# Token stages: centring and variance as 64x64 blocks, one paired hidden bank, more PSUM banks in the second stage, and other piece orders on TensorE and ScalarE

## The chip, the cores and the metric

The kernel is one program on one core of a Trainium2 chip. The metric is device time in microseconds (us) for one execution, lower is better. The engines are TensorE (PE; its weight loads are PEld), VectorE (DVE), ScalarE (ACT), GpSimd (POOL) and SyncE (SP, which here only issues DMAs). Each engine runs its own instructions in order; semaphores join them.

## The reference

An image tensor x of 4 images, 48 channels, 128 x 128 pixels goes through two layers. Each has a convolution part and then a feed-forward part on tokens (a token is the 48 channels of one pixel):

```python
x = x + _L0_conv_ref(_ln_c(x), ...)
t = _to_tokens(x)
t = t + _L0_ffn_ref(_ln_t(t), L0_ffn_W1, L0_ffn_b1, L0_ffn_W2, L0_ffn_b2)
x = _from_tokens(t, x)
x = x + _L1_conv_ref(_ln_c(x), ...)
t = _to_tokens(x)
t = t + _L1_ffn_ref(_ln_t(t), L1_ffn_W1, L1_ffn_b1, L1_ffn_W2, L1_ffn_b2)

def _ln_t(v, eps=1e-05):
    m = jnp.mean(v, axis=-1, keepdims=True)
    s = jnp.var(v, axis=-1, keepdims=True)
    return (v - m) / jnp.sqrt(s + eps)
def _qlinear(x, W, b):
    y = q_acc(jnp.einsum('bsk,nk->bsn', q_mul(x), q_mul(W)))   # inputs rounded to 5/2-bit floats
    return q_acc(y + q_mul(b))                                 # sums rounded to 5/10-bit floats
# feed-forward: y = _qlinear(relu(_qlinear(x, W1, b1)), W2, b2), 48 -> 192 -> 48
```

## The kernel before

The program runs stages one after another: an expansion, a gated convolution, **token stage 0** (`mix0`), a wavelet part, attention maps, a fusion part, and **token stage 1** (`mix1`). Both token stages are the function `token_mix`. Each ends a convolution (projection and residual), normalises, runs the feed-forward, and stage 0 also makes the channel norm (`_ln_c`) that the next convolution reads. Stage 0 is called with a 96-channel source and is `wide`; stage 1 isn't. Stage 0 lies at about 806 to 1262 us of the span, stage 1 at 2171 to 2534.

A token stage has 64 steps (`2 * N`). A step holds 512 tokens of two images: 48 channels of one image on partitions 0 to 47, of the other on 64 to 111, with a gap of zeros between (`CP` is 112, `PADH` is 64, `NT` is 512, `HID` is 96). A step's work is cut into pieces, and the pieces of a step belong to different pipeline stages. The function `staged` writes each engine's queue: in iteration k it emits, in the order of the list `pieces`, the piece (s, f) for step k - s. So the list is at once a software pipeline and a fixed queue order. The pieces of a step m are:

- `project` (PE, L876/L879 in stage 0, L882 in stage 1) into `x1_bank`, and `add_residual` (DVE, L1034/L1036 or L1039), pipeline stage 0
- `centre_in` (PE, L888: multiply by a matrix that subtracts the mean) and `square("in")` (ACT, L951), stage 0
- `variance("in")` (PE, L906: multiply the squares by a matrix that averages), `root("in")` (ACT: Ln, L958, then Exp, L961), and `quantize_norm` (DVE, L1047: makes the fp8 tile `xq`), stage 1
- `hide(0)`, `hide(1)` (PE, L919: each half of the 192 hidden units, for both images), `round_hidden(0)`, `round_hidden(1)` (ACT, L968: PSUM to the fp16 tile `h16`), `bias_hidden` (DVE, L1053, twice: `hb`), `quantize_hidden` (DVE, L1063: the fp8 tile `hq`), stage 2
- `show` (PE, L931) and `round_shown` (ACT, L974: tile `y`), `add_shown` (DVE, L1069, L1074) and the store, stage 3 in token stage 0 and 4 in token stage 1
- only in token stage 0: `centre_out` (PE, L894) and `square("out")` at 4, `variance("out")`, `root("out")` and `normalise` (DVE, L1083) at 5

An f32 matmul is two MATMUL instructions in the trace, an fp8 matmul one. In the first token stage the bank that `project` fills, `x1_bank`, is also the bank of the variance, and the bank of `show` is that of the outer variance; in the second, `x1_bank` is shared in the same way. So `project` waits on `logged["in"]` (the Ln has read the variance). The hidden banks are two in stage 0 and four in stage 1.

At a stage's start DVE zeroes tiles (L984 to L998) and then sets `prepared`, on which SP waits with its weight loads; after those come the first steps.

The queue order of DVE is in both versions

```python
pieces = [(0, add_residual), (SHOWN, add_shown), (2, bias_hidden), (2, quantize_hidden), (1, quantize_norm)]
if norm_dst is not None:
    pieces.append((5, normalise))
```

## Time and profile before

| what | value |
|---|---|
| runs | 2534.08, 2541.41, 2864.81 us; median 2541.41 |
| profiled execution, own time | 2536.14 us |
| its span | 2534.40 us (1.7 us lie around it) |
| mean granted PE clock | 0.935 of 2.4 GHz |
| busy over the span | PE 2148.1 us, DVE 1439.6, ACT 1151.7, POOL 532.4 |
| token stage 0, 806 to 1262 us | PE 418.5 us busy, ACT 389.0, DVE 347.4 |
| token stage 1, 2171 to 2534.4 us | PE 312.3 us busy, ACT 270.5, DVE 282.1 |

Busy time counts overlapped instructions once. "Idle before" is what an engine waited for in front of an instruction, and what ended the wait. The granted clock is in parts of 2.4 GHz, and has two levels, 1.0 and 0.5.

### The profile page before, as it was taken

What the parts mean: (1) busy time and instruction counts of PE and PEld (TensorE: products, weight loads), DVE (VectorE), ACT (ScalarE), POOL (GpSimd) and SP (SyncE); (2) the same over time, 40 slices, a digit from 0 to 9 for tenths busy, and PEclk for the clock granted to TensorE, in tenths of its full rate; (3) what the DMA queues carried; (4) which work ended last, traced back from release to release, by engine and by line L of the source; (5) the groups of instructions that cost most, each with busy time, mean ns of one, the idle gap of its engine ahead of it and who ended that gap; (6) DMA issues with size and microseconds to landing.
All of it is one profiled execution on the core that took longest, in us unless ns stands there. A gap on an engine that the chain in (4) does not pass through costs nothing. (4 is left out here: it accounts for less than half of the span.)

```text
span 2534.4 us, 69339 instructions
## 1 busy us (share of the span) xinstructions
PE 2148.1 (85%) x25034; PEld 1260.1 (50%) x25034; DVE 1439.6 (57%) x2567; ACT 1151.7 (45%) x2290; POOL 532.4 (21%) x912
## 2 busy tenths in 40 slices
PE   7679949998996999999879999999936777688887
PEld 3345517766784333333346666666614545233332
DVE  3345501111112777777657888787834445588887
ACT  4346522222222888888722323232201111477776
...
GB/s 154 262 256 269 247 295 282 263 264 228 255 216 97 130 150 144 151 141 154 101 113 133 126 134 129 130 129 130 113 112 271 250 247 175 87 112 108 109 110 84
DMA packets 559393, 434.57 MB, mean 171 GB/s; under 512 B 363592, under 2 KB 498432, under 8 KB 555878
## 3 DMA queue, kind: packets, MB, share of 16 engines
...
q8 instruction: 129, 2.11, 0.4%
...
## 5 line engine op out<-in xcount | busy, mean ns | idle before, releaser
L615 PE MATMUL gate_ps<-gate_data,gate_wt 64*64 64x289 f32 x6144 | 391.2, 411 | 29.4 <-issue 22.2
L615 PEld LDWEIGHTS gate_ps<-gate_data,gate_wt 64*64 64x64 f32 x6144 | 307.6, 134 | 114.1 <-issue 45.8
L676 DVE TENSOR_TENSOR gate_out<-gate_gelu,gate_ps 128x578 f32<-128x578 f32 x96 | 72.2, 756 | 375.4 <-PE gate_ps L615 327.1
L968 ACT CAST mix_h<-mix_bank 96x512 f16<-96x512 f32 x512 | 267.6, 592 | 10.3 <-PE mix_bank L919 6.4
L2076 PE MATMUL fus_bank<-fus_xt,fus_taps 64*32 64x256 f32 x3840 | 139.9, 422 | 78.1 <-issue 55.0
L653 ACT ACTIVATE gate_gelu<-gate_ps 128x578 f32<-128x578 f32 x96 | 62.7, 653 | 300.7 <-PE gate_ps L615 275.1
L1053 DVE TENSOR_SCALAR mix_hb<-mix_h,mix_b1q 96x1024 f16<-96x1024 f16 x256 | 122.7, 479 | 98.0 <-ACT mix_h L968 98.0
L919 PE MATMUL mix_bank<-mix_xq,mix_w1q 112*96 112x512 fp8e5 x512 | 143.1, 381 | 34.3 <-ACT mix_h L968 23.0
L1063 DVE CAST mix_hq<-mix_hb 96x2048 fp8e5<-96x2048 f16 x128 | 156.5, 1223 | 21.1 <-DVE mix_hb L1053 19.2
L292 DVE COPY exp_out<-exp_y 128x384 f32<-128x384 f32 x192 | 102.3, 566 | 104.3 <-PE exp_y L255 54.1
L255 PE MATMUL exp_y<-exp_win,exp_xb 48*128 48x192 f32 x1024 | 117.8, 368 | 47.8 <-DVE exp_out L292 29.7
L2076 PEld LDWEIGHTS fus_bank<-fus_xt,fus_taps 64*32 64x32 f32 x3840 | 88.5, 117 | 123.5 <-issue 107.4
L931 PE MATMUL mix_x_bank<-mix_hq,mix_w2q 96*112 96x512 fp8e5 x512 | 135.6, 387 | 6.5 <-DVE mix_hq L1063 4.4
L255 PEld LDWEIGHTS exp_y<-exp_win,exp_xb 48*128 48x128 f32 x1024 | 92.5, 205 | 87.8 <-ACT exp_out L292 52.3
L888 PE MATMUL mix_centre_in<-mix_x,mix_center 112*112 112x512 f32 x256 | 134.3, 607 | 2.1 <-DVE mix_x L1036 1.2
L882 PE MATMUL mix_x_bank<-mix_sc,mix_proj 112*112 112x512 f32 x128 | 86.4, 757 | 58.3 <-ACT mix_logv_in L958 36.8
L906 PE MATMUL mix_x_bank<-mix_sq_in,mix_average 112*112 112x512 f32 x256 | 132.8, 601 | 2.1 <-DVE mix_x L1036 1.2
...
L974 ACT CAST mix_y<-mix_x_bank 112x512 f16<-112x512 f32 x128 | 74.9, 585 | 119.1 <-PE mix_x_bank L931 119.1
L1622 ACT ACTIVATE wav_sg<-wav_small_bank,tab_levels 128x4 f32<-128x4 f32 x48 | 12.7, 264 | 250.7 <-PE wav_small_bank L1527 250.7
L2104 ACT ACTIVATE fus_gate<-fus_bank,fus_bias 128x512 f32<-128x512 f32 x24 | 16.5, 687 | 226.9 <-PE fus_bank L2085 226.9
L1483 PE MATMUL wav_front<-wav_strips,wav_front_w 48*32 48x256 f32 x3840 | 117.0, 382 | 0.0
...
## 6 DMA issues: line engine op xcount, KB each, us to landing
...
```

Of the source, the lines that this page charges most:

```text
L255: mm = pe.matmul(ps_y[h][q % 2][:, O2 * x:O2 * (x + 1)], xb[u][rows, 2 * q + x].rearrange("c s y x -> c (s y x)"), win[rows, :], start=Tru ...
L292: copy(out[u][h][:, :, 2 * q:2 * q + 2], ps_y[h][p][:, 0:2 * O2].rearrange("p (x c) -> p c x", x=2)).then_inc(emptied[h][p], 1)
L615: mm = pe.matmul(banks(a, v)[64 * g:64 * (g + 1), r], wt[q][64 * r:64 * (r + 1), 2 * a + g, n, :], src, start=n == 0, stop=n == 3)
L888: pe.matmul(centre_bank["in"][at.pair][0:CP, :], center[:, :], x1[at.slot][:, :], start=True, stop=True).then_inc(centered["in"], 1)
L906: pe.matmul(var_bank[v][0:CP, :], average[:, :], sq[v][at.pair][:, :], start=True, stop=True).then_inc(var[v], 1)
L919: pe.matmul(bank[(2 * m + h) % len(bank)][0:HID, :], w1q[:, h, m, :], xq[at.pair][:, :], start=True, stop=True).then_inc(hidden, 1)
L931: mm = pe.matmul(x2_bank[0:CP, :], w2q[:, h, m, :], hq[at.pair][:, m, h, :], start=(h + m == 0), stop=(h + m == 2))
L968: act.copy(h16[at.pair][:, m, h, :], bank[(2 * m + h) % len(bank)][0:HID, :]).then_inc(h16_ready, 1)
L1053: relu = dve.tensor_scalar(hb[at.pair][:, m, :, :].rearrange("p h n -> p (h n)"), h16[at.pair][:, m, :, :].rearrange("p h n -> p (h n)"), ...
L1063: dve.tensor_copy(hq[at.pair][:, :, :, :].rearrange("p m h n -> p (m h n)"), hb[at.pair][:, :, :, :].rearrange("p m h n -> p (m h n)"), sa ...
L1483: x = pe.matmul(half(u, r, 0, Q0)[to:to + STRIP], front_w[u][64 * r:64 * r + K0, 5 + dx, :], strips[u][64 * r:64 * r + K0, g, :, dx:dx + S ...
L2076: mm = pe.matmul(part(u, 0)[STRIP * g:STRIP * (g + 1), r], taps[u][rows, ch, m, :], xt[u][rows, ch, g, :, m:m + S0], start=n == 0, stop=n ...
```

## The change

In `token_mix` only:

1. Centring and variance are block-diagonal: the 112x112 matmul becomes two 64x64 matmuls, one for each image, on tiles of the PE array. Centring exchanges the halves (rows 0-63 write partitions 64-127 and the reverse), variance does not, so the two use all four tiles between them. Operand tiles grow to 128 partitions, and the added rows are zeroed once at the start; the fp8 matmuls take 128 rows.
2. `hide(m)` writes both images into one pair of banks, `pair_bank`, for m = 0 and for m = 1. ACT copies them as one 96x1024 instruction. `hide(1)` waits until the copy of `hide(0)` is done, in both stages.
3. Stage 1 has two projection banks and a bank of its own for the variance. `project` there waits on `x1_ready` and not on the Ln; `variance("in")` waits for the Ln of the step before.
4. The order of pieces changes on PE and ACT, in both stages. DVE and SP keep theirs.
5. `show` in stage 0 waits for one Ln of the outer norm more (`n + 2`), and the outer variance for one `y` less.

```diff
-        x1_bank, x2_bank = k.ps("x1_bank"), k.ps("x2_bank")
-        var_bank = {"in": x1_bank, "out": x2_bank}
-        bank = [k.ps(f"bank{j}") for j in range(8 - 2 - 2 * len(norms))]
+        x1_banks, x2_bank = [k.ps(f"x1_bank{u}") for u in range(1 if wide else 2)], k.ps("x2_bank")
+        var_bank = {"in": x1_banks[0], "out": x2_bank} if wide else {"in": k.ps("var_bank")}
+        pair_bank = k.ps("pair_bank", (128, 2 * NT))
...
-                    pe.wait_ge(logged["in"], at.n + 1)
+                    if wide:
+                        pe.wait_ge(logged["in"], at.n + 1)
+                    elif not isinstance(at.n, int) or at.n >= 2:
+                        pe.wait_ge(x1_ready, at.n - 1)
...
+                def exchange(v, at, x):
+                    pe.sem_inc(pe_turn, 1)
+                    pe.matmul(centre_bank[v][at.pair][PADH:128, :], center[0:PADH, 0:PADH], x[0:PADH, :], start=True, stop=True)
+                    pe.matmul(centre_bank[v][at.pair][0:PADH, :], center[PADH:128, PADH:128], x[PADH:128, :],
+                              start=True, stop=True).then_inc(centered[v], 1)
...
-                            pe.wait_ge(y16_ready, capped(at.n + 3, 2 * N) + 1)
+                            pe.wait_ge(y16_ready, capped(at.n + 2, 2 * N) + 1)
...
-                        pe.matmul(var_bank[v][0:CP, :], average[:, :], sq[v][at.pair][:, :],
+                        pe.sem_inc(pe_turn, 1)
+                        pe.matmul(var_bank[v][0:PADH, :], average[0:PADH, 0:PADH], sq[v][at.pair][0:PADH, :], start=True, stop=True)
+                        pe.matmul(var_bank[v][PADH:128, :], average[PADH:128, PADH:128], sq[v][at.pair][PADH:128, :],
                                   start=True, stop=True).then_inc(var[v], 1)
...
-                        if m == 1 and len(bank) == 2:
-                            pe.wait_ge(h16_ready, 4 * at.n + 2)
+                        if m == 1:
+                            pe.wait_ge(h16_ready, 2 * at.n + 1)
...
-                            pe.matmul(bank[(2 * m + h) % len(bank)][0:HID, :], w1q[:, h, m, :], xq[at.pair][:, :],
-                                      start=True, stop=True).then_inc(hidden, 1)
+                            mm = pe.matmul(pair_bank[0:HID, NT * h:NT * (h + 1)], w1q[:, 1 - h, m, :],
+                                           xq[at.pair][:, :], start=True, stop=True)
+                        mm.then_inc(hidden, 1)
...
-                        pe.wait_ge(logged["out"], at.n + 1)
+                        pe.wait_ge(logged["out"], at.n + 2)
...
-                pieces = [(0, project), (SHOWN, show), (2, hide(0)), (2, hide(1)), (1, variance("in")), (0, centre_in)]
+                pieces = [(0, project), (2, hide(0)), (SHOWN, show), (1, variance("in")), (2, hide(1)), (0, centre_in)]
                 if norm_dst is not None:
-                    pieces = [(0, project), (3, show), (2, hide(0)), (4, centre_out), (2, hide(1)), (1, variance("in")), (5, variance("out")), (0, centre_in)]
+                    pieces = [(0, project), (5, variance("out")), (2, hide(0)), (3, show), (4, centre_out), (1, variance("in")), (2, hide(1)), (0, centre_in)]
...
-                        for h in range(2):
-                            act.wait_ge(hidden, 4 * at.n + 2 * m + h + 1)
-                            act.copy(h16[at.pair][:, m, h, :], bank[(2 * m + h) % len(bank)][0:HID, :]
-                                     ).then_inc(h16_ready, 1)
+                        act.wait_ge(hidden, 2 * at.n + m + 1)
+                        act.copy(h16[at.pair][:, m, :, :].rearrange("p h n -> p (h n)"), pair_bank[0:HID, :]
+                                 ).then_inc(h16_ready, 1)
...
-                pieces = [(SHOWN, round_shown), (2, round_hidden(0)), (2, round_hidden(1)), (1, root("in")),
-                          (0, square("in"))]
+                pieces = [(2, round_hidden(0)), (SHOWN, round_shown), (1, root("in")), (2, round_hidden(1)), (0, square("in"))]
                 if norm_dst is not None:
-                    pieces = [(3, round_shown), (2, round_hidden(0)), (4, square("out")), (2, round_hidden(1)), (1, root("in")), (5, root("out")), (0, square("in"))]
+                    pieces = [(5, root("out")), (2, round_hidden(0)), (3, round_shown), (4, square("out")), (1, root("in")), (2, round_hidden(1)), (0, square("in"))]
...
+                dve.memset(center[:, :], 0.0)
+                dve.memset(average[:, :], 0.0)
+                for x in x1 + x2 + xq:
+                    dve.memset(x[96:128, :], 0.0)
+                for x in hq:
+                    dve.memset(x[96:128].rearrange("p m h n -> p (m h n)"), 0.0)
```

## Rows read from the trace of the kernel before

**Rows 1.** The chain that ended last, 2200 to 2534 us, its shares by line

```profile
by line: ACT mix_h L968 30.5%; PE mix_x_bank L882 23.1%; PE mix_x_bank L931 15.9%; issue 14.5%; ACT mix_logv_in L958 10.2%; ACT mix_y L974 1.3%; ACTq L967 1.2%; DVE mix_hq L1063 0.7%; DVE mix_hb L1053 0.4%; DVE mix_xq L1047 0.4%; PE mix_ban
```

**Rows 2.** Windows: length, busy PE, PEld, DVE, ACT, POOL, granted clock, DMA share, GB/s

```profile
806.00:1262.00 456.00, 418.45 (x1522) 171.96 (x1522) 347.43 (x573) 389.04 (x698) 0.00 (x0) 0.99 0.73 139
2171.00:2534.40 363.40, 312.25 (x896) 123.81 (x896) 282.11 (x448) 270.54 (x512) 0.00 (x0) 0.97 0.40 103
2510.00:2520.00 10.00, 8.22 (x28) 3.57 (x28) 7.80 (x13) 7.94 (x16) 0.00 (x0) 1.00 0.16 45
2520.00:2530.00 10.00, 4.14 (x13) 1.62 (x12) 6.63 (x12) 4.54 (x9) 0.00 (x0) 0.70 0.14 40
```

**Rows 3.** Timeline, token stage 0, PE: start, length, line, tiles, [idle before <- releaser]

```profile
1004.11 0.60 PE L919 MATMUL mix_bank<-mix_xq,mix_w1q 112*96 112x512 fp8e5 x2 [0.44 <-ACT mix_h L968]
...
1005.41 1.02 PE L906 MATMUL mix_x_bank<-mix_sq_out,mix_average 112*112 112x512 f32 x2
1006.27 1.02 PE L888 MATMUL mix_centre_in<-mix_x,mix_center 112*112 112x512 f32 x2
1007.22 0.98 PE L876 MATMUL mix_x_bank<-mix_sc,mix_proj 96*48 96x448 f32 x4
```

**Rows 4.** Timeline, token stage 0, ACT, one step

```profile
1002.41 0.58 ACT L974 CAST mix_y<-mix_x_bank 112x512 f16<-112x512 f32 x1 [0.67 <-PE mix_x_bank L931]
...
1009.35 0.58 ACT L974 CAST mix_y<-mix_x_bank 112x512 f16<-112x512 f32 x1 [0.67 <-PE mix_x_bank L931]
```

**Rows 5.** Timeline, token stage 1, PE

```profile
2354.67 1.03 PE L931 MATMUL mix_x_bank<-mix_hq,mix_w2q 96*112 96x512 fp8e5 x4
2355.54 1.03 PE L919 MATMUL mix_bank<-mix_xq,mix_w1q 112*96 112x512 fp8e5 x4
...
2358.90 1.33 PE L882 MATMUL mix_x_bank<-mix_sc,mix_proj 112*112 112x512 f32 x2 [0.61 <-ACT mix_logv_in L958]
2360.06 1.03 PE L931 MATMUL mix_x_bank<-mix_hq,mix_w2q 96*112 96x512 fp8e5 x4
```

**Rows 6.** Timeline, token stage 1, ACT

```profile
2355.74 0.58 ACT L974 CAST mix_y<-mix_x_bank 112x512 f16<-112x512 f32 x1 [1.14 <-PE mix_x_bank L931]
2356.22 2.04 ACT L968 CAST mix_h<-mix_bank 96x512 f16<-96x512 f32 x4
2358.13 0.72 ACT L958 ACTIVATE mix_logv_in<-mix_x_bank,mix_eps 112x512 f32<-112x512 f32 x1
2358.88 0.63 ACT L961 ACTIVATE mix_rstd_in<-mix_logv_in 112x512 f32<-112x512 f32 x1
```

**Rows 7.** Timeline, last steps of token stage 1, PE, ACT and DVE

```profile
2517.29 1.03 PE L919 MATMUL mix_bank<-mix_xq,mix_w1q 112*96 112x512 fp8e5 x4 [1.77 <-DVE mix_xq L1047]
...
2517.71 2.04 ACT L968 CAST mix_h<-mix_bank 96x512 f16<-96x512 f32 x4 [0.89 <-PE mix_bank L919]
...
2519.78 0.48 DVE L1053 TENSOR_SCALAR mix_hb<-mix_h,mix_b1q 96x1024 f16<-96x1024 f16 x1 [0.49 <-ACT mix_h L968]
...
2520.45 1.22 DVE L1063 CAST mix_hq<-mix_hb 96x2048 fp8e5<-96x2048 f16 x1 [0.18 <-DVE mix_hb L1053]
...
2521.59 0.68 DVE L1047 TENSOR_TENSOR mix_xq<-mix_centre_in,mix_rstd_in 112x512 fp8e5<-112x512 f32 x1
...
2522.42 1.03 PE L919 MATMUL mix_bank<-mix_xq,mix_w1q 112*96 112x512 fp8e5 x4 [2.37 <-DVE mix_xq L1047]
```

**Rows 8.** Groups by form: line, tiles, count, busy us, mean ns, idle before

```profile
L615 PE MATMUL gate_ps<-gate_data,gate_wt 64*64 64x289 f32 x6144 | 391.2, 411 | 29.4 <-issue 22.2 <-ACT gate_wt L648 4.1 <-DVE gate_out L676 3.1
L968 ACT CAST mix_h<-mix_bank 96x512 f16<-96x512 f32 x512 | 267.6, 592 | 10.3 <-PE mix_bank L919 6.4
L637 ACT ACTIVATE gate_stage<-gate_ps,gate_maps 96x1024 f32<-96x1024 f32 x10 | 10.2, 1107 | 5.9 <-PE gate_ps L578 5.9
L629 ACT ACTIVATE gate_hid<-gate_ps,gate_maps 128x512 f32<-128x512 f32 x2 | 1.4, 687 | 8.9 <-PE gate_ps L568 8.9
L993 DVE MEMSET mix_rs<- 32x512 f32 x4 | 1.9, 485 | 0.5
```

More of the change, by code:

```diff
@@ L721, in token_mix @@
         rs = [k.sb(f"rs{u}", [CP, NT]) for u in U]
-        x1 = [k.sb(f"x1{u}", [CP, NT]) for u in range(KEPT)]
+        x1 = [k.sb(f"x1{u}", [128, NT]) for u in range(KEPT)]
         norms = ("in", "out") if norm_dst is not None else ("in",)
-        sq, logv, rstd = ({v: [k.sb(f"{name}_{v}{u}", [CP, NT]) for u in U] for v in norms}
+        sq, logv, rstd = ({v: [k.sb(f"{name}_{v}{u}", [128, NT]) for u in U] for v in norms}
                           for name in ("sq", "logv", "rstd"))
-        xq = [k.sb(f"xq{u}", [CP, NT], F8) for u in U]
+        xq = [k.sb(f"xq{u}", [128, NT], F8) for u in U]
         h16 = [k.sb(f"h16{u}", [HID, 2, 2, NT], F16) for u in U]
         hb = [k.sb(f"hb{u}", [HID, 2, 2, NT], F16) for u in U]
-        hq = [k.sb(f"hq{u}", [HID, 2, 2, NT], F8) for u in U]
+        hq = [k.sb(f"hq{u}", [128, 2, 2, NT], F8) for u in U]
         y16 = [k.sb(f"y16{u}", [CP, NT], F16) for u in U]
         yb = [k.sb(f"yb{u}", [CP, NT], F16) for u in U]
-        x2 = [k.sb(f"x2{u}", [CP, NT]) for u in U]
+        x2 = [k.sb(f"x2{u}", [128, NT]) for u in U]
         xn = [k.sb(f"xn{u}", [CP, 4 * 2 * XW]) for u in U] if norm_dst is not None else None
@@ L838, in store_norm @@
                     for h in range(2):
-                        rows = slice(PADH * h, PADH * h + C)
+                        rows = slice(PADH * (1 - h), PADH * (1 - h) + C)
                         def keep(y, first, n):
@@ L893, in centre_out @@
                     pe.wait_ge(xn_ready, at.n + 1)
-                    pe.matmul(centre_bank["out"][at.pair][0:CP, :], center[:, :], x2[at.pair][:, :],
-                              start=True, stop=True).then_inc(centered["out"], 1)
+                    exchange("out", at, x2[at.pair])
                 def variance(v):
                     def piece(at):
-                        if v == "in":
+                        if v == "in" and not wide:
+                            pe.wait_ge(logged["in"], at.n + FREE["in"])
+                        elif v == "in":
                             pe.wait_ge(x1_ready, capped(at.n + 2, 2 * N))
                         else:
-                            pe.wait_ge(y16_ready, capped(at.n + 3, 2 * N) + 1)
+                            pe.wait_ge(y16_ready, capped(at.n + 2, 2 * N) + 1)
                             if isinstance(at.n, int):
@@ L950, in piece @@
                         act.wait_ge(centered[v], at.n + 1)
-                        act.activation(sq[v][at.pair][:, :], centre_bank[v][at.pair][0:CP, :], ACT.Square).then_inc(squared[v], 1)
+                        act.activation(sq[v][at.pair][:, :], centre_bank[v][at.pair][:, :], ACT.Square).then_inc(squared[v], 1)
                     return piece
@@ L957, in piece @@
                         act.wait_ge(var[v], at.n + 1)
-                        act.activation(logv[v][at.pair][:, :], var_bank[v][0:CP, :], ACT.Ln,
+                        act.activation(logv[v][at.pair][0:CP, :], var_bank[v][0:CP, :], ACT.Ln,
                                        bias=eps[0:CP, m:m + 1]).then_inc(logged[v], 1)
                         act.wait_ge(logged[v], at.n + 1 + FREE[v])
-                        act.activation(rstd[v][at.pair][:, :], logv[v][at.pair][:, :], ACT.Exp, scale=-0.5).then_inc(rooted[v], 1)
+                        act.activation(rstd[v][at.pair][0:CP, :], logv[v][at.pair][0:CP, :], ACT.Exp, scale=-0.5).then_inc(rooted[v], 1)
                     return piece
@@ L997, in _ @@
                         dve.memset(sc[u][0][32:64, :], 0.0)
-                dve.memset(x1_bank[32:64, :], 0.0).then_inc(prepared, 1)
+                for x in x1_banks:
+                    last = dve.memset(x[32:64, :], 0.0)
+                last.then_inc(prepared, 1)
                 dve.wait_ge(weights_in, 16 * (9 if wide else 12))
@@ L1032, in outer @@
                             return x[:, :].rearrange("c (y v x) -> c y v x", y=4, x=P8)[:, :, :, 0]
-                        dve.tensor_tensor(inner(x1[at.slot]), x1_bank[0:CP, 0:cut].rearrange(
+                        dve.tensor_tensor(inner(x1[at.slot][0:CP]), x1_banks[0][0:CP, 0:cut].rearrange(
                             "c (y x v) -> c y x v", y=4, v=BX), inner(rs[at.pair]), ALU.add)
-                        add = dve.tensor_tensor(outer(x1[at.slot]), x1_bank[0:CP, cut:NT].rearrange(
+                        add = dve.tensor_tensor(outer(x1[at.slot][0:CP]), x1_banks[0][0:CP, cut:NT].rearrange(
                             "c (y v) -> c y v", v=BX), outer(rs[at.pair]), ALU.add)
                     else:
-                        add = dve.scalar_tensor_tensor(out=x1[at.slot][:, :], in0=x1_bank[0:CP, :],
+                        add = dve.scalar_tensor_tensor(out=x1[at.slot][0:CP, :], in0=x1_banks[at.pair][0:CP, :],
                                                        scalar=pbias[0:CP, 0:1], in1=rs[at.pair][:, :],
@@ L1062, in quantize_hidden @@
                     dve.sem_inc(dve_turn, 1)
[L1063 removed]
+                    dve.tensor_copy(hq[at.pair][0:HID].rearrange("p m h n -> p (m h n)"),
                                     hb[at.pair][:, :, :, :].rearrange("p m h n -> p (m h n)"), saturate=False
```

30 lines of the change are left out of this document (14 added, 16 removed).

## Prediction

> **What bounds the kernel now.** I began with the busy time in windows [rows 2]. In token stage 0 PE is busy 418 of 456 us and ACT 389; in token stage 1 PE 312 of 363, DVE 282, ACT 271. No engine is full, so each stage runs at the length of a closed loop of waits, and the reader should look for the idle time that comes back in every step. A step of stage 0 lasts 1009.35 - 1002.41 = 6.94 us [rows 4]; 64 of them are 444 us. In each, PE idles 0.44 us for ACT's copy of the hidden half [rows 3] and ACT 0.67 us for `show` [rows 4]. A step of stage 1 lasts 2360.06 - 2354.67 = 5.39 us [rows 5], in all 345 us. There `project` waits 0.61 us for the Ln [rows 5], because the two share a bank, and ACT waits 1.14 us for `show` [rows 6]. The chain of waits names that loop: copies of the hidden half 30.5%, `project` 23.1%, `show` 15.9%, Ln 10.2% [rows 1].
>
> **A second loop, close behind.** The last steps of stage 1 have no `project` left, so they show what comes next [rows 7]: hide starts at 2517.29 and again at 2522.42, 5.13 us apart, and what it waited for is `xq`. The loop is: hide to first copy 0.42; four copies 2.04; 0.03; first `hb` start to `hq` start 0.67; `hq` to `xq` 1.14; `xq` to the next hide 0.83. It sums to 5.13. It is closed because DVE's queue has `xq` of step m+1 behind `hb` and `hq` of step m, and the change leaves DVE's queue alone. So in stage 1 this loop had 0.26 us of slack; removing the first loop alone buys at most that.
>
> **Part 1, removed waits.** In stage 1 `project` no longer waits for the Ln. The gain is 0.26 us a step, 17 us in all, if the second loop stays at 5.13. In stage 0 that wait stays.
>
> **Part 2, the paired copy.** Four copies of 512 become two of 1024. From 512 to 1024 columns an ACTIVATE grows from 687 to 1107 ns [rows 8], 420 ns. A 592 ns copy [rows 8] becomes 1.01 us. The next ACT instruction starts some 0.10 us before an end (2355.74 + 0.58 against 2356.22 [rows 6]). Two pairs cost 2.04 now and 1.93 then: ACT gains 0.1 us a step. In exchange a copy waits for both matmuls, 0.22 us more (half of the 0.43 that a hide of two takes, 0.87 for four [rows 5]).
>
> **Part 3, tiles.** Two 64x64 matmuls replace one 112x112, each as long as before (0.86 us from 1005.41 to 1006.27 [rows 3]). Side by side the pair costs 0.86, in turn 1.72. The gate convolution also uses 64x64 tiles: 6144 instructions in 391 us [rows 8], 64 ns each, where 289 columns at the pace of the centring (512 in 0.43) last 242 ns. So nearly four tiles run at once there, and I take side by side; that also lets the outer centring and the inner variance overlap in stage 0. A change of array shape costs 0.10 us: `centre_in` to `project` takes 0.95 where like shapes take 0.86 [rows 3]. Stage 0 goes from two changes to six. These terms matter only where they lie on the loop.
>
> The Trainium skill, TensorEngine Tiling, Restrictions and Gotchas, Gotcha 1, speaks against this: different row tiles cannot access the same PSUM bank simultaneously, and here both halves of a pair write one bank. No row here shows two row tiles in one bank. By that rule the sum is that of the second rival below.
>
> **Part 4, the orders.** This decides. The second copy, on which `hb` waits, moved behind the root on ACT, while `hide(1)` moved behind `show` and the variance on PE. I walk the second loop again, with 0 at the start of `hide(0)`.
>
> Stage 1: two matmuls, so the copy starts at 0.42 [rows 7] + 0.22 = 0.64 and lasts 1.01, ACT is free at 1.55. `show` starts at 0.43, its result is read at 0.43 + 1.07 = 1.50 (2354.67 to 2355.74 [rows 5, 6]), so `y` runs from 1.55 and ACT is free at 2.03. The variance starts at 0.43 + 0.87 + 0.10 = 1.40 and can be read 1.07 later, so the Ln starts at 2.47. Ln to Exp takes 0.75 (2358.13 to 2358.88), Exp to the next 0.63 - 0.10 = 0.53 [rows 6]: the second copy starts at 3.75 and ends at 4.76. `hide(1)` was done by 2.9. Then as now 0.03 + 0.67 + 1.14 + 0.83 = 2.67 to the next hide [rows 7]. The loop is 7.4 us where the step now takes 5.39. PE has only about 4.9 us of work in it (`project` 1.16 [rows 5], hides 0.87, `show` 0.87, two pairs 1.72, changes 0.3) and can't shorten it.
>
> Stage 0: copy from 0.64 to 1.65. `show`, then a change: centring starts at 1.40, read at 2.47. `y` is over before; the outer square runs from 2.47 (0.53 to the next), Ln from 3.0 (variance beside the centring, ready by then), Exp, second copy at 3.0 + 0.75 + 0.53 = 4.28, end 5.29, and 2.67 behind it: 7.9 to 8.0. I take 7.9 against 6.94. The new `show` wait on the outer Ln doesn't bind: that Ln is first on ACT, its variance right behind `project`, before a hide that waits for `xq`. Behind the waiting hide on PE stand `show`, both norms and `centre_in`; ACT's copy waits for it and so does everything behind that.
>
> **Sum.** Stage 1: 64 x (7.4 - 5.39) = 129 us. Stage 0: 64 x (7.9 - 6.94) = 61 us. The zeroing lies in front of the weight loads, which wait for it, so nothing hides it. A 32x512 MEMSET takes 485 ns [rows 8], some 0.55 with what follows. Stage 0 adds eight of that size (`x1`, `x2`, two `hq` of 2048 bytes), stage 1 thirteen (eight `x1`, `x2`, `hq`, one bank); the fp8 `xq` and the two matrices are a quarter of it, four in each stage: 21 x 0.55 + 8 x 0.15 = 13 us. The clock: stage 1 will have one PE gap of some 2.3 us a step. In the tail of before, gaps of 1.77 and 2.37 [rows 7] lie in a window granted 1.00 and the next is 0.70 [rows 2], one level of 2.4 and one of 1.2 GHz. A fall in a step doubles hide, `show` and variance, up to 2.2 us. Between none and all 64 steps that is 0 to 140 us; since a single gap of 2.37 did not bring it down at once, I take 10. The sum against the profiled 2536.1 is 2536 + 129 + 61 + 13 + 10 = 2749 us; the median of the runs lies 5 above the profiled one, so 2754.
>
> **Rivals.**
> - *The clock falls in most steps of stage 1.* For it: the 0.70 window [rows 2]. Against it: gaps of 2 us are filled in both neighbours by 4.9 us of work. 48 steps x 2.0 = 96 us in place of 10: 2840.
> - *The two tiles of a pair take turns.* For it: no row has that case. Against it: the gate's tiles [rows 8], and `project`'s four instructions of 448 columns in 0.98 us [rows 3] where in turn they need 1.5, though those halves differ in columns only. Stage 1: the variance is ready 0.86 later, 8.3 us a step. Stage 0: centring and variance in turn, ready at 3.3 and 5.0, then Ln, Exp, copy and the rest, about 10.0. 64 x (2.9 + 3.1) = 384 us in place of 190: 2948.
> - *Faster: the second loop doesn't close.* If ACT's second copy ended within 2.7 us of `hide(0)`'s start in stage 1, as the four copies do now (2.46 [rows 7]), the stage would be limited by PE at 4.9 and stage 0 by ACT at 6.94 - 0.67 - 0.1 = 6.2. 64 x (0.5 + 0.75) = 79 us less and 13 for the zeroing: 2475. It needs Ln, Exp and `y`, 1.8 us, off the way between the two copies. The printed order puts them there, so this is only a misreading of the queue.
> - *Within 2%*: the loop closes, but steps overlap more than my walk allows by half or more in both stages.
>
> **How the numbers follow.** Forecast 0.68, clock 0.12, turns 0.10, faster 0.06, within 2% 0.04. Two percent is 51 us, which is about what a measurement of this kernel can tell from no change (two runs of before lie 7 us apart, one 320 above). The forecast's own range is 2715 to 2795, from 0.3 us a step either way in 128 steps; to hold 8 in 10 it reaches over the clock rival: 2690 to 2855. Slower 0.90, within 2% 0.04, faster 0.06.
>
> **What would show each step.** In stage 1, hides `hide(0)` to `hide(0)` 7.4 us apart, each released by `xq`, with PE idle some 2.3 us; `hb`'s second half waiting about 1 us or more for the copy; the copy at 1.01 us. In stage 0, 7.9 us a step, also released by `xq`. No wait of `project` on the Ln in stage 1. Centring, two tiles, in about 1.1 us in all, not 1.9. The granted clock of stage 1 tells the first rival. The prediction is wrong if DVE isn't what `hide(0)` waits for, or if the gap between the two copies on ACT is far from 2.1 us.

## The result, and the profile after

| kernel | median us | runs |
|---|---|---|
| before | 2537.74 | 2527.68 to 2864.81, 4 runs |
| after | 2758.23 | 2754.97 to 2765.58, 4 runs |

The ratio is 1.0892, with a 95% interval of 1.0857 to 1.0927. The change makes the kernel 8.9% slower. One run of before, at 2864.81 us, lies 13% above its other three, and the ratio leaves it out. The profiled execution of after took 2754.97 us, its span 2753.2: 218.8 us more than the span of before.

I place that difference by counting steps. A step is the distance between two `y` copies on ACT; "typical" is the median distance, "mean" is first `y` to last `y` over 63, the shorter last steps included. The two differ where some steps are held up and others are not.

| | stage 0 typical / mean | stage 1 typical / mean |
|---|---|---|
| before | 6.93 / 6.91 us | 5.39 / 5.32 us |
| after | 7.89 / 8.05 us | 7.43 / 7.56 us |

First `y` to last `y` is 506.9 us in stage 0 of after (825.69 to 1332.62), 435.1 before: 72 more. In stage 1 it is 476.2 (2271.49 to 2747.70) against 335.1: 141 more. The wait in front of a stage's first `project` grew by 5.4 us in stage 0 and 7.6 us in stage 1 (from 19.34 and 21.51 to the 24.75 and 29.07 below). Sum 226; the other stages came out 7 us shorter.

Windows of after, over both token stages and over one typical step of stage 1 (columns as in [rows 2]):

```profile
800.00:1330.00 530.00, 412.99 (x2028) 128.38 (x2028) 340.47 (x569) 376.95 (x568) 0.00 (x0) 0.97 0.64 120
2250.00:2753.00 503.00, 365.46 (x1148) 100.86 (x1146) 281.21 (x447) 270.64 (x384) 0.00 (x0) 0.93 0.28 73
2454.99:2462.42 7.43, 5.30 (x18) 1.51 (x19) 4.40 (x8) 4.20 (x6) 0.00 (x0) 1.00 0.31 83
```

Against [rows 2]: ACT's and DVE's busy time in stage 1 is what it was (270.5 and 282.1), while the stage is 140 us longer. These two got no more work; they wait. PE's busy time rose from 312 to 365 us, for changes of array shape and matmuls at the lower clock, and still PE is idle for 138 of 503 us. The third line shows how much: in a step of 7.43 us PE works 5.30, DVE 4.40, ACT 4.20.

Timeline of after, PE: the first `project` of each stage, some of stage 0, and one step of stage 1. It answers to [rows 3] and [rows 5]:

```profile
802.72 1.73 PE L879 MATMUL mix_x_bank<-mix_sc,mix_proj 96*48 96x448 f32 x4 [24.75 <-DMA mix_sc<-g]
...
1059.60 0.64 PE L891 MATMUL mix_centre_out<-mix_x,mix_center 64*64 64x512 f32 x1
1059.60 0.64 PE L892 MATMUL mix_centre_out<-mix_x,mix_center 64*64 64x512 f32 x1
1059.77 0.61 PE L916 MATMUL mix_x_bank<-mix_sq_in,mix_average 64*64 64x512 f32 x1
1059.77 0.64 PE L917 MATMUL mix_x_bank<-mix_sq_in,mix_average 64*64 64x512 f32 x1
...
1066.09 0.60 PE L930 MATMUL mix_pair_bank<-mix_xq,mix_w1q 128*96 128x512 fp8e5 x2 [1.65 <-DVE mix_xq L1065]
...
1071.78 0.98 PE L879 MATMUL mix_x_bank<-mix_sc,mix_proj 96*48 96x448 f32 x4 [1.41 <-DMA mix_sc<-g]
...
2245.52 2.02 PE L885 MATMUL mix_x_bank<-mix_sc,mix_proj 112*112 112x512 f32 x2 [29.07 <-DMA mix_sc<-mixed]
...
2454.99 0.60 PE L930 MATMUL mix_pair_bank<-mix_xq,mix_w1q 128*96 128x512 fp8e5 x2 [2.13 <-DVE mix_xq L1065]
2455.43 1.03 PE L943 MATMUL mix_x_bank<-mix_hq,mix_w2q 128*112 128x512 fp8e5 x4
2456.39 0.64 PE L916 MATMUL mix_var_bank<-mix_sq_in,mix_average 64*64 64x512 f32 x1
...
2457.39 0.63 PE L930 MATMUL mix_pair_bank<-mix_xq,mix_w1q 128*96 128x512 fp8e5 x2
2457.96 0.64 PE L891 MATMUL mix_centre_in<-mix_x,mix_center 64*64 64x512 f32 x1
...
2458.96 1.33 PE L885 MATMUL mix_x_bank<-mix_sc,mix_proj 112*112 112x512 f32 x2
2462.42 0.60 PE L930 MATMUL mix_pair_bank<-mix_xq,mix_w1q 128*96 128x512 fp8e5 x2 [2.13 <-DVE mix_xq L1065]
```

In the last line the reader is to see the loop closing: PE has been idle for 2.13 us, and what it waited for is `xq`. `project` (2458.96) no longer waits for the Ln, as the change intends [rows 5]. Where that 7.43 us goes is on ACT (answering to [rows 6]) and on DVE (answering to [rows 7]):

```profile
2455.63 1.01 ACT L979 CAST mix_h<-mix_pair_bank 96x1024 f16<-96x1024 f32 x1 [2.81 <-PE mix_pair_bank L930]
2456.54 0.58 ACT L985 CAST mix_y<-mix_x_bank 112x512 f16<-112x512 f32 x1
2457.51 0.69 ACT L970 ACTIVATE mix_logv_in<-mix_var_bank,mix_eps 112x512 f32<-112x512 f32 x1 [0.39 <-PE mix_var_bank L917]
2458.23 0.63 ACT L973 ACTIVATE mix_rstd_in<-mix_logv_in 112x512 f32<-112x512 f32 x1
2458.77 0.99 ACT L979 CAST mix_h<-mix_pair_bank 96x1024 f16<-96x1024 f32 x1
...
2459.79 0.48 DVE L1071 TENSOR_SCALAR mix_hb<-mix_h,mix_b1q 96x1024 f16<-96x1024 f16 x1 [1.16 <-ACT mix_h L979]
...
2460.45 1.22 DVE L1081 CAST mix_hq<-mix_hb 96x2048 fp8e5<-96x2048 f16 x1 [0.18 <-DVE mix_hb L1071]
2461.60 0.68 DVE L1065 TENSOR_TENSOR mix_xq<-mix_centre_in,mix_rstd_in 112x512 fp8e5<-112x512 f32 x1
```

From the second `hide` (2457.39) on, its bank could be copied at 2458.03, but ACT starts at 2458.77, since Ln and Exp are ahead of it in the queue and the Ln waits for the variance. Measured from 2454.99, the chain stands at 0.64 (first copy), 1.55 (`y`), 2.52 (Ln), 3.78 (second copy), 4.80 (`hb`), 5.46 (`hq`), 6.61 (`xq`), 7.43 (next `hide`).

### The profile page after: what moved, and what is told of

Same layout as the page of the kernel before. It is cut to its first block and busy times, and to the rows that moved or that the text cites. A ratio compares the mean times of both kernels' runs of the same rounds, so it can differ in the third digit from the quotient of the medians.

```text
span 2753.2 us, 70702 instructions
## 1 busy us (share of the span) xinstructions
PE 2193.6 (80%) x25802; PEld 1201.5 (44%) x25802; DVE 1451.6 (53%) x2596; ACT 1141.8 (41%) x2034; POOL 531.6 (19%) x912
## 5 line engine op out<-in xcount | busy, mean ns | idle before, releaser
L615 PEld LDWEIGHTS gate_ps<-gate_data,gate_wt 64*64 64x64 f32 x6144 | 315.6, 134 | 101.1 <-issue 40.7
L979 ACT CAST mix_h<-mix_pair_bank 96x1024 f16<-96x1024 f32 x256 | 255.4, 998 | 221.8 <-PE mix_pair_bank L930 221.8
L930 PE MATMUL mix_pair_bank<-mix_xq,mix_w1q 128*96 128x512 fp8e5 x512 | 166.3, 408 | 207.3 <-DVE mix_xq L1065 206.6
L930 PEld LDWEIGHTS mix_pair_bank<-mix_xq,mix_w1q 128*96 128x96 fp8e5 x512 | 43.5, 124 | 444.6 <-issue 444.5
L943 PE MATMUL mix_x_bank<-mix_hq,mix_w2q 128*112 128x512 fp8e5 x512 | 139.0, 396 | 6.4 <-DVE mix_hq L1081 3.5
L891 PE MATMUL mix_centre_in<-mix_x,mix_center 64*64 64x512 f32 x256 | 140.8, 631 | 2.3 <-DVE mix_x L1054 1.3
L892 PE MATMUL mix_centre_in<-mix_x,mix_center 64*64 64x512 f32 x256 | 140.9, 631 | 0.0
L1087 DVE TENSOR_SCALAR mix_yb<-mix_y,mix_b2q 112x512 f16<-112x512 f16 x128 | 45.1, 353 | 166.6 <-ACT mix_y L985 166.6
```

The lines of the kernel that those rows point to most:

```text
L615: mm = pe.matmul(banks(a, v)[64 * g:64 * (g + 1), r], wt[q][64 * r:64 * (r + 1), 2 * a + g, n, :], src, start=n == 0, stop=n == 3)
L891: pe.matmul(centre_bank[v][at.pair][PADH:128, :], center[0:PADH, 0:PADH], x[0:PADH, :], start=True, stop=True)
L892: pe.matmul(centre_bank[v][at.pair][0:PADH, :], center[PADH:128, PADH:128], x[PADH:128, :], start=True, stop=True).then_inc(centered[v], 1)
L930: mm = pe.matmul(pair_bank[0:HID, NT * h:NT * (h + 1)], w1q[:, 1 - h, m, :], xq[at.pair][:, :], start=True, stop=True)
L943: mm = pe.matmul(x2_bank[0:CP, :], w2q[:, h, m, :], hq[at.pair][:, m, h, :], start=(h + m == 0), stop=(h + m == 2))
L979: act.copy(h16[at.pair][:, m, :, :].rearrange("p h n -> p (h n)"), pair_bank[0:HID, :]).then_inc(h16_ready, 1)
```

## The experiments

Their steps and times; the ratio is to the runs of before on the same chip. e1 to e4 ran on one chip (before 2536.20 us there), e5 to e9 on a second (2531.43), e10 to e13 on a third (2538.49), so times of different groups are compared by their ratios or by their steps. The kernels e5, e6 and e11 ran once and have no interval. The intervals of e2, e3 and e12 lie clear of 1 but reach over 2%.

| kernel | stage 0 typical / mean | stage 1 typical / mean | us | ratio |
|---|---|---|---|---|
| e1_xq_before_hq | 7.25 / 7.95 | 6.03 / 5.95 | 2646.65 | 1.0432 (1.0380 to 1.0483) |
| e2_xq_first | 7.08 / 7.95 | 5.13 / 5.07 | 2588.85 | 1.0211 (1.0153 to 1.0269) |
| e3_old_orders | 6.55 / 6.90 | 6.11 / 6.11 | 2596.75 | 1.0234 (1.0185 to 1.0283) |
| e4_tiles_only | 6.61 / 6.92 | 5.39 / 5.32 | 2542.36 | 1.0029 (1.0005 to 1.0053) |
| e5_extra_ahead | 10.0 / 9.74 | 8.97 / 8.72 | 2939.37 | |
| e6_extra_behind | 8.24 / 8.30 | 7.43 / 7.62 | 2780.73 | |
| e8_xq_first_late_store | 7.26 / 7.23 | 5.13 / 5.07 | 2543.7 | 1.0052 (1.0036 to 1.0068) |
| e9_tiles_late_store | 6.61 / 6.59 | 5.39 / 5.33 | 2525.76 | 0.9977 (0.9959 to 0.9996) |
| e10_before_late_store | 6.93 / 6.88 | 5.39 / 5.32 | 2532.93 | 0.9975 (0.9953 to 0.9998) |
| e11_ahead_project_twice | 10.0 / 9.78 | 9.11 / 8.87 | 2954.85 | |
| e12_best_old_stage0 | 6.55 / 6.54 | 4.80 / 4.82 | 2479.99 | 0.9774 (0.9746 to 0.9802) |
| e13_new_stage0 | 6.03 / 6.03 | 4.80 / 4.79 | 2442.6 | 0.9631 (0.9598 to 0.9664) |

**e1 and e2: take `hq`, then `hb` too, off the loop.** Both are after with another queue order on DVE. In e2 `hide` also waits until ACT has copied the bank's earlier contents, which in after follows from `xq`.

```diff
 # e1
-pieces = [(0, add_residual), (SHOWN, add_shown), (2, bias_hidden), (2, quantize_hidden), (1, quantize_norm)]
+pieces = [(0, add_residual), (SHOWN, add_shown), (2, bias_hidden), (1, quantize_norm), (2, quantize_hidden)]
 # e2
+pieces = [(0, add_residual), (SHOWN, add_shown), (1, quantize_norm), (2, bias_hidden), (2, quantize_hidden)]
 # e2, in hide(0)
+elif not isinstance(at.n, int) or at.n >= 1:
+    pe.wait_ge(h16_ready, 2 * at.n)
```

Expected of e1:

> The changed kernel with one edit: on DVE xq of the next step is made ahead of the hidden cast hq of this one. Loop theory (hide, copy, root, copy, hb, hq, xq, hide): the loop loses hq's 1.14 us and the 0.2 us that hq waits for hb, so stage 1 goes from 7.43 to about 6.0 us a step, and stage 0 from 8.0 to 7.2 to 7.4; in all 2755 - 64 x (1.4 + 0.6 to 0.8) = 2615 to 2630 us. Rival, tiles and changes of array shape on PE: no piece of PE changes, so 2755 stays. Rival, the shared pair of banks: the two hides and the two copies are as before, so 2755 stays.

Expected of e2:

> The changed kernel with xq of the next step ahead of both hb and hq on DVE, and a wait of hide(0) for the second copy of the step before, which was implied until now. Loop theory: what is left of the loop is hide, copy, root, copy, hide: 4.8 us in stage 1, where PE's own work of about 4.9 to 5.0 then sets the step; stage 0 about 7.1. In all 2755 - 64 x (2.45 + 0.9) = 2540 us, so as fast as the kernel before. Rival, tiles on PE: 2755. Rival, the shared pair of banks: 2755 or more, since one more wait on it is written out.

Timeline of e1, PE, stage 1:

```profile
2401.32 0.60 PE L930 MATMUL mix_pair_bank<-mix_xq,mix_w1q 128*96 128x512 fp8e5 x2 [0.73 <-DVE mix_xq L1065]
...
2407.35 0.60 PE L930 MATMUL mix_pair_bank<-mix_xq,mix_w1q 128*96 128x512 fp8e5 x2 [0.73 <-DVE mix_xq L1065]
```

One swap on DVE takes 1.40 us off a step: PE's idle time falls by the same amount, 2.13 to 0.73. `xq` now starts 0.41 us behind `hb` where it started 1.81 behind it (2461.60 - 2459.79): the 1.15 of `hq`, and the 0.25 that `hq` waits for `hb` and `xq` doesn't. In e2 nothing is left of the loop in stage 1. Windows of e2:

```profile
2380.00:2500.00 120.00, 120.00 (x424) 36.77 (x420) 100.71 (x164) 98.19 (x142) 0.00 (x0) 1.00 0.43 115
```

PE is busy for 120.00 of 120 us and the step is 5.13, PE's own work. Neither PE's nor ACT's order was touched, so the loss of stage 1 is the loop through DVE's queue, and nothing else. But both kernels came out above what was expected of them (2646.65 against 2615 to 2630, 2588.85 against 2540), because stage 0 took 7.95 us a step in the mean. Its steps alternate there, in e2 6.95 and mostly 8.7 to 9.5 us, and the median (7.25, 7.08) lies at the short ones. Something else holds stage 0. Timeline of e2, stage 0, all engines:

```profile
1056.02 0.98 PE L879 MATMUL mix_x_bank<-mix_sc,mix_proj 96*48 96x448 f32 x4 [1.46 <-DMA mix_sc<-g]
...
1059.11 1.04 PE L945 MATMUL mix_x_bank<-mix_hq,mix_w2q 128*112 128x512 fp8e5 x4 [0.43 <-ACT mix_logv_out L972]
1060.32 0.58 ACT L987 CAST mix_y<-mix_x_bank 112x512 f16<-112x512 f32 x1
1060.93 0.35 DVE L1089 TENSOR_SCALAR mix_yb<-mix_y,mix_b2q 112x512 f16<-112x512 f16 x1 [1.90 <-ACT mix_y L987]
1061.51 0.69 DVE L1094 TENSOR_TENSOR mix_x<-mix_yb,mix_x 112x512 f32<-112x512 f16 x1 [0.22 <-DVE mix_yb L1089]
1062.37 0.86 SPq L834 DMA_DIRECT2D x<-mix_x  x2
...
1063.51 0.88 SPq L843 DMA_DIRECT2D xp<-mix_xn  x2
1064.59 0.34 SPq L801 DMA_DIRECT2D mix_sc<-g  x1
...
1072.18 1.36 PE L879 MATMUL mix_x_bank<-mix_sc,mix_proj 96*48 96x448 f32 x4 [1.70 <-DMA mix_sc<-g]
```

Read downwards it is a third loop. `project` (1056.02) holds up `show`, since the outer variance stands behind it on PE (1057.05), ACT's Ln reads that (1058.17), and `show` waits 0.43 us for the Ln. That is the wait that the change added; it costs 1.0 us in all in stage 0 of after, but 9.2 us in e2, both between 830 and 1240 us. SP issues, in a fixed order, the stores of `x` and `xp` and then the next source load. The store waits for `add_shown` (`mix_x`, 1062.20), so the load of a later source is issued only at 1064.59, takes 7.6 us to land and be seen, and `project` (1072.18) waits for it. From `project` to that `project` are 16.16 us. One load brings the source of two steps: 8.08 us a step. The waits of e2 between 830 and 1240 us add `project`'s up to (total, times, longest):

```profile
PE mix_x_bank L879 <- DMA mix_sc<-g: 36.0, 25, 1.9
```

After has the same wait (24.7 us in 22 waits between 830 and 1240 us; the line at 1071.78 above is one).

**e8, e9, e10: move the store behind in SP's queue.** In e2, e4 (below) and before, `store_x2` of token stage 0 goes one pipeline stage later.

```diff
-staged(sp, 2 * N, KEPT, [(0, load), (SHOWN + 1, store_x2)] + [(7, store_norm)] * wide, LEAD)
+staged(sp, 2 * N, KEPT, [(0, load), (SHOWN + (2 if wide else 1), store_x2)] + [(7, store_norm)] * wide, LEAD)
```

> e2_xq_first with one edit: in stage 0, SP's store of x2 is one iteration later in its queue (stage 5 for stage 4), so that the load of the next source tile is not queued behind a store that waits for y. New theory for stage 0 (third loop, over two steps: project, show, y, x2, SP's stores, source load 7.5 us, project): stage 0 goes from 7.95 to about 7.1 us a step, 50 us less than e2_xq_first, near 2538 us; stage 1 stays at 5.13. Rival, DMA bandwidth bounds stage 0 (busy share 0.65): nothing changes, 2589. Rival, the later store delays DVE's next x2: slower than e2_xq_first.

> e4_tiles_only with the same later store of x2. In e4_tiles_only most steps of stage 0 take 6.61 us, but the mean is 6.92, with waits for the source load. Third-loop theory: the mean comes down to about 6.6, 64 x 0.3 = 20 us less than e4_tiles_only, near 2522 us, a little faster than the kernel before. Rival, DMA bandwidth: it stays at 2542.

> The kernel before with the later store of x2 in stage 0 alone. If the source load is only just in time before (issued at 1013.82, landing 7.2 us later, project at 1021.1), its other loop (copy of the hidden half, y) sets 6.93 us a step: no change, 2531 us, within 0.3%. Rival: the store is what holds stage 0 before too: up to 0.3 us a step, 20 us faster.

In e8 the wait of `project` on the load is gone, and the mean step falls from 7.95 to 7.23; the steps no longer alternate, and the typical one is 7.26. That is 45 us in 63 steps; the ratios, 1.0211 and 1.0052, say 40. In e9 the mean goes from 6.92 to 6.59. In e10, before with the late store, it goes from 6.91 to 6.88 only, 2 us in all: before's loop of 6.94 us [rows 4] was just as long as this one, so shortening one of them was worth next to nothing there. What sets the 7.26 us of e8, 0.33 over before, was not taken apart.

The third loop was there before, hidden, and the change lengthened it to 8 us. In before the load is issued 6.60 us after `project` (1007.22 in [rows 3]):

```profile
1013.82 0.34 SPq L801 DMA_DIRECT2D mix_sc<-g  x1
```

In e2 it is issued 8.57 us after it (1056.02 to 1064.59), 2 us more for two steps. `show` starts 1.0 us behind `project` in before and 3.1 in e2, with the outer variance, a `hide` and the wait for the Ln between them. With the orders and waits of before and the new tiles (e3, e4) the mean is 6.90 and 6.92; no run parts the order on PE from that on ACT and from the added wait.

**e3: the old orders with the new tiles and banks.** After, with the lists of PE and ACT from before and their waits.

```diff
 # PE, stage 1
-pieces = [(0, project), (2, hide(0)), (SHOWN, show), (1, variance("in")), (2, hide(1)), (0, centre_in)]
+pieces = [(0, project), (SHOWN, show), (2, hide(0)), (2, hide(1)), (1, variance("in")), (0, centre_in)]
 # ACT, stage 1
-pieces = [(2, round_hidden(0)), (SHOWN, round_shown), (1, root("in")), (2, round_hidden(1)), (0, square("in"))]
+pieces = [(SHOWN, round_shown), (2, round_hidden(0)), (2, round_hidden(1)), (1, root("in")), (0, square("in"))]
...
```

> The changed kernel with the piece orders of before on PE and ACT, and the two waits that belong to them; 64x64 blocks, pair of banks, bank split of stage 1 stay. Loop theory: the copies are close together again. Stage 1: PE waits in hide(1) for the first copy, so the loop is copy, hide, copy, hb, hq, xq, hide: 6.2 us a step (7.43 in the changed kernel, 5.39 before). Stage 0 about 7.0. In all 2755 - 64 x (1.2 + 1.0) = 2615 us. Rival, tiles and shape changes: it stays near 2755. Rival, shared pair: it keeps most of the loss, and in stage 0 too.

Timeline of e3, PE, stage 1:

```profile
2400.00 0.60 PE L930 MATMUL mix_pair_bank<-mix_xq,mix_w1q 128*96 128x512 fp8e5 x2 [0.57 <-DVE mix_xq L1065]
2401.80 0.60 PE L930 MATMUL mix_pair_bank<-mix_xq,mix_w1q 128*96 128x512 fp8e5 x2 [1.19 <-ACT mix_h L979]
...
2406.11 0.60 PE L930 MATMUL mix_pair_bank<-mix_xq,mix_w1q 128*96 128x512 fp8e5 x2 [0.57 <-DVE mix_xq L1065]
```

Back to back, the second `hide` has to wait 1.19 us until ACT has read the one pair of hidden banks: 1.80 from `hide` to `hide`, 0.64 to the copy, 1.01 of copy, 2.67 to the next `hide` [rows 7], which is 6.12; measured 6.11. So the old orders are better than the new ones here by 1.3 us, and still worse than before by 0.7 because of the single pair. Stage 0, which had two hidden banks already, gains 0.38 in the typical step but nothing in the mean (6.90), since every second step waits for its source load.

**e4: only the tiles.** Before, with the 64x64 blocks, the 128-row operands and the zeroing; the edit in words:

```diff
-centre and variance: one 112x112 matmul
+centre: two 64x64 matmuls that exchange the halves; variance: two that don't
+dve.memset of the added rows; w1q[:, 1 - h], 128-row fp8 operands
```

> The kernel before with the 64x64 blocks, 128-row operands and their zeroing alone; banks, 512-column copies and orders are those of before. Loop theory: only changes of array shape that lie on a loop count, 0.1 us each: none in stage 1 (5.4 us a step), one in stage 0 (7.0), and 13 us for the zeroing: 2537 + 13 + 6 = 2556 us, within 1% of before. Rival, tiles are what costs: most of the 217 us, over 2650.

The typical step of stage 0 was 6.61, shorter than the 7.0 expected; PE's timeline in e4 says why:

```profile
1000.80 0.64 PE L911 MATMUL mix_x_bank<-mix_sq_in,mix_average 64*64 64x512 f32 x1
1000.81 0.64 PE L912 MATMUL mix_x_bank<-mix_sq_in,mix_average 64*64 64x512 f32 x1
1000.83 0.64 PE L888 MATMUL mix_centre_in<-mix_x,mix_center 64*64 64x512 f32 x1
1000.84 0.64 PE L889 MATMUL mix_centre_in<-mix_x,mix_center 64*64 64x512 f32 x1
...
1001.71 0.59 PE L911 MATMUL mix_x_bank<-mix_sq_out,mix_average 64*64 64x512 f32 x1
```

The queue holds inner variance, outer variance, inner centring. The centring, on the two tiles that the variances do not use, runs with the inner variance, 0.03 us behind it, and the outer variance, which stands ahead of it in the queue, follows 0.88 us later. All regular steps of e4 have this, with 0.76 to 0.88 us between the two. Three pairs take the time of two. The gain of 0.32 a step is then lost to the source load (mean 6.92), and stage 1 is unchanged, its loops being elsewhere. What is left of e4 against before is the zeroing: 13 us by the waits, 1 to 13 by the ratio. e9, without the third loop, should be 63 x (6.88 - 6.59) = 18 us faster than e10 by its steps, less 13 of zeroing; the ratios (0.9977 and 0.9975, each about 0.002 either way) cannot tell the 5 us that are left from nothing.

**e5 and e6: one more DVE instruction, in the loop or behind it.** A second copy of `xq`'s instruction writes to a tile that nobody reads, ahead of `xq` (e5) or right behind it (e6). All other work is that of after.

```diff
+spare = k.sb("spare", [128, NT], F8)
 ...
+dve.tensor_tensor(spare[0:CP, :], centre_bank["in"][at.pair][0:CP, :], rstd["in"][at.pair][0:CP, :], ALU.mult, saturate=False)
```

> The changed kernel with one DVE instruction more in each step: the operation that makes xq is done once more into a spare tile, directly ahead of xq. Loop theory: the instruction lies on the loop in stage 1, so the step grows by its 0.60 us, from 7.43 to 8.03. Stage 0 grows too, by 0.3 to 0.6. In all 2755 + 38 + 20 to 38 = 2810 to 2830 us. Rival, the load of stage 1 on DVE as a whole or PE's tiles set the step: DVE is busy under 60% there, so nothing is added, or as much as in e6_extra_behind.

> The changed kernel with the same extra DVE instruction directly behind xq. Loop theory: in stage 1 PE has xq already and goes on, and DVE waits over 1 us later in the step anyway, so the step stays at 7.43. In stage 0 it delays the residual add and the store, so 0 to 0.4 us a step. In all 2755 to 2780 us. Rival, DVE's load as a whole: the same growth as e5_extra_ahead.

DVE is busy 4.40 of 7.43 us, so a theory of busy time says that neither costs anything. Behind `xq` (e6), stage 1 keeps its 7.43, and stage 0 grows by 0.35 in the typical step. Ahead of it, the step at full clock is 8.02. Timeline of e5, PE:

```profile
2514.78 0.60 PE L931 MATMUL mix_pair_bank<-mix_xq,mix_w1q 128*96 128x512 fp8e5 x2 [2.56 <-DVE mix_xq L1068]
...
2515.22 1.03 PE L944 MATMUL mix_x_bank<-mix_hq,mix_w2q 128*112 128x512 fp8e5 x4
...
2522.80 0.69 PE L931 MATMUL mix_pair_bank<-mix_xq,mix_w1q 128*96 128x512 fp8e5 x2 [2.73 <-DVE mix_xq L1068]
2523.29 1.91 PE L944 MATMUL mix_x_bank<-mix_hq,mix_w2q 128*112 128x512 fp8e5 x4
...
2532.47 0.60 PE L931 MATMUL mix_pair_bank<-mix_xq,mix_w1q 128*96 128x512 fp8e5 x2 [2.73 <-DVE mix_xq L1068]
```

0.59 us more, as `xq` itself needs from start to next start (2461.60 to 2462.20). But two steps in three of e5, from `hide` to `hide`, are like the second one, 9.1 to 9.7 us, with `show` and its neighbours at half pace (1.91 us where the step before has 1.03). So the expectation of 2810 to 2830 us failed: against the profiled run of after the kernel lost 184 us and not the 75 that 128 x 0.59 makes. Windows of e5, stage 1:

```profile
2400.00:2920.00 520.00, 365.75 (x1049) 97.16 (x1048) 290.74 (x466) 249.31 (x353) 0.00 (x0) 0.88 0.24 65
```

The granted clock is 0.88 against after's 0.93, and 0.85 between 850 and 1240 us of stage 0, against 0.99. In stage 1 the rest of the loss is that: the first rival of the prediction, real in this kernel. In stage 0 the typical step grew from 7.89 to 10.0, and how much of that is the clock was not measured apart.

**e11: fill the gap.** e5, with `project` of stage 1 issued twice into the same bank with the same values.

```diff
-mm = pe.matmul(x1_banks[at.pair][0:CP, :], proj[:, :], ...)
+for _ in range(2):
+    mm = pe.matmul(x1_banks[at.pair][0:CP, :], proj[:, :], ...)
```

> e5_extra_ahead with the projection matmul of stage 1 issued twice (the second writes the same values over the first): 1.16 us more work for PE in each step, in its idle gap of 2.7 us. Clock theory: e5_extra_ahead lies over its walk (8.03 us a step in stage 1, most steps measured about 9.0) because PE falls to 1.2 GHz after that gap in nearly every step. With the gap filled to about 1.6 us the granted clock of stage 1 rises from 0.88 to over 0.97 and the mean step falls from 8.72 to about 8.1, 40 us less in all, near 2900 us, although PE does more. Rival, the extra length of e5_extra_ahead has another cause, such as DVE or a bank: no change, 2939, or 64 x 1.16 = 74 us more if PE's work lies on the loop.

Timeline of e11, PE, and its window of stage 1:

```profile
2611.99 0.60 PE L932 MATMUL mix_pair_bank<-mix_xq,mix_w1q 128*96 128x512 fp8e5 x2 [1.65 <-DVE mix_xq L1069]
...
2620.01 1.06 PE L932 MATMUL mix_pair_bank<-mix_xq,mix_w1q 128*96 128x512 fp8e5 x2 [1.65 <-DVE mix_xq L1069]
```

```profile
2400.00:2920.00 520.00, 424.68 (x1143) 120.94 (x1141) 287.52 (x460) 243.48 (x343) 0.00 (x0) 0.88 0.24 65
```

The gap is 1.65, shorter than after's 2.13, PE is busy 425 of 520 us, and the clock is still 0.88. The expectation, over 0.97 and near 2900 us, failed. So the length of this gap alone is not what decides. What makes the clock fall in most steps here, and in about every fourth step of stage 1 in after, stays open.

**e12 and e13: a version that beats both.** e12 is e3's stage 0 (tiles, the old queue orders) with the late store; in stage 1 after's banks and orders with `xq` first on DVE as in e2, and 112x112 blocks without zeroing. e13 is e12 with stage 0 written anew:

```diff
 # PE, stage 0
-[(0, project), (3, show), (2, hide(0)), (4, centre_out), (2, hide(1)), (1, variance("in")), (5, variance("out")), (0, centre_in)]
+[(5, variance("out")), (4, centre_out), (0, project), (2, hide(0)), (3, show), (2, hide(1)), (1, variance("in")), (0, centre_in)]
 # ACT, stage 0
+[(5, root("out")), (2, round_hidden(0)), (4, square("out")), (3, round_shown), (2, round_hidden(1)), (1, root("in")), (0, square("in"))]
 # DVE, stage 0
+[(0, add_residual), (5, normalise), (3, add_shown), (2, bias_hidden), (1, quantize_norm), (2, quantize_hidden)]
```

> A kernel put together from what the runs showed. Stage 0: 64x64 blocks, paired copies, the piece orders of before and the later store (6.55 us a step in most steps of e3_old_orders). Stage 1: pair of banks, bank split and piece orders of the change, xq first on DVE, but 112x112 matmuls and no zeroing for them, so four changes of array shape less, 0.2 to 0.3 us of PE's 5.13 us in e2_xq_first: 4.85 to 4.95 us. In all 2531 + 13 - 7 - 64 x (0.38 + 0.5) = 2481 us, 2% faster than before. Rival, the loops of stage 0 come back through the DMA queue: 2505.

> e12_best_old_stage0 with other orders in stage 0. PE: outer variance, outer centring, project, hide(0), show, hide(1), inner variance, inner centring. ACT: outer root, copy, outer square, y, copy, inner root, inner square. DVE: residual add, normalise, add of y, hb, xq, hq. Both pairs of norms overlap on PE's tiles; by the walk the engines allow 6.0 us a step. The source load allows about 9.7 us and SP's issues for two steps, some 6.2 a step. So 6.2 to 6.6 us: 2465 to 2481 us. Rival, y is late for the store and the load: slower than e12_best_old_stage0.

e12 takes 2480.0 us (0.9774), as expected; e13 takes 2442.6 us (0.9631, 0.9598 to 0.9664), better than the 2465 to 2481 expected, because its stage 0 runs at 6.03 us a step and not at 6.2 to 6.6. In stage 1 the step is 4.80, 0.33 less than e2's 5.13: the same orders without tiles. There PE is the bound, and four changes of array shape less give about 0.1 each; the fp8 operands have fewer rows there too, which no run parts from it. Windows of e13:

```profile
820.00:1215.00 395.00, 366.30 (x2008) 122.44 (x2000) 334.94 (x568) 370.78 (x571) 0.00 (x0) 0.99 0.83 158
2120.00:2440.00 320.00, 303.93 (x888) 118.49 (x886) 275.32 (x446) 268.22 (x383) 0.00 (x0) 0.99 0.43 115
```

In stage 1 PE is nearly full, in stage 0 PE and ACT are both over 90% busy: little is left for the loops to cost.

## Why the prediction was right

It said 2754 in a range of 2690 to 2855; measured 2758.23. That the two are 4 us apart is partly luck: in the sum below, terms that came out too small and 7 us that nobody explained cancel. The mechanism, though, is the one it named. By its own steps:

- *The second loop.* The walk of stage 1 had 0.64, 1.55, 2.47, 3.75, the `hb` at 4.79 and 7.4 at the end; the trace has 0.64, 1.55, 2.52, 3.78, 4.80 and 7.43. e1, e2, e5 and e6 show in stage 1 that it is the loop: what is taken off its path comes off the step, an instruction added on it comes on in full, and beside it costs nothing. Its term of 129 us holds (63 x 2.04). PE's own work, put at 4.9 us a step, is 5.13 in e2; it lay under the loop and did not count.
- *Part 1.* Right, and worth nothing in this order: `project` lost its wait and started none of the work earlier that counts. Whether the separate bank pays where the second loop is cut (e2, e12) no run shows by itself.
- *Part 2.* The paired copy was put at 1.01; the mean of 256 is 0.998. What it costs beside its length was seen only partly: a single pair of banks makes `hide` wait for the copy as soon as the two are near each other (1.19 us in e3). The new order hides this.
- *Part 3.* Both halves of a pair start together, 0.01 us apart in most steps and 0.04 at most, though both write one bank, each its own partitions: `mix_x_bank` at 1059.77, and `mix_var_bank`, where the whole pair takes 1.00 with its change of shape (2456.39 to 2457.39). Centring, two tiles, takes 1.00 (2457.96 to 2458.96), predicted 1.1. In stage 0 outer centring and inner variance, four tiles, take 1.17 together (1059.60 to 1060.77). The Trainium skill, TensorEngine Tiling (Array Packing), Restrictions and Gotchas, Gotcha 1, says that different row tiles cannot access the same PSUM bank simultaneously. The trace does not agree: here they do, and the pair takes 1.00 us and not the 1.7 of two in turn.
- *Stage 0, the term that was mis-sized.* "I take 7.9": the typical step is 7.89, but the mean is 8.05, and 72 us came instead of 61. What was missing in the walk is the third loop, through SP's queue. The prediction weighed the wait of `show` on the outer Ln, rightly for after, and named what stands behind it on PE and ACT. It did not follow `show` through `y`, `x` and the store to the source load. In after the second loop hides most of it (8.05, against 7.95 where the second loop is cut), which is why the miss stayed small. After itself was not run with the late store, so that the source loads are what is over 7.89 is read from the waits. In e1 and e2 it took nearly all that stage 0 would have gained: mean 7.95 where e8 has 7.23.
- *The zeroing.* 13 us predicted, 5.4 + 7.6 = 13.0 measured in the waits in front of the first `project`.
- *The clock, the other term that was mis-sized.* "I take 10": of the first 60 steps of stage 1, 15 take 8.4 us, and some beside them 0.1 to 0.4 us more than 7.43; together 17 us over 60 x 7.43. "Between none and all" was fair: e5 has the clock low in most steps. But the reason for taking so few was a misreading: only the gap of 1.77 lies in the window granted 1.00. The gap of 2.37 ends at 2522.42 [rows 7], in the window granted 0.70 [rows 2], and in the trace of before the clock is at 1.00 up to 2523.9 and at 0.5 from there. So the fall came 1.5 us behind that gap.
- *The rivals.* The clock in most steps: not here. Taking turns: refuted by the starts and lengths above. The second loop not closing: refuted by the 2.13 us that `hide` waits for `xq` in the steps of stage 1. Within 2%: refuted by the interval of the ratio.
- *The sum.* In stage 1, 63 x 2.04 = 129, 17 of clock, and 4 to 5 less because the last steps, which have no work behind them, are shortened by more than in before: 141. In stage 0, 63 x 0.96 = 60 and 11 over it, most of it for the source loads: 72 with rounding. With 13 of zeroing 226; the span grew by 218.8. The 7 us less lie outside the two stages, and no run tells why. Against the predicted growth of 213, stage 0 gave 11 more, stage 1 with its clock 2 more, and the rest 7 less.
